# Two of four Hadamard fold quarters from sums and differences formed on VectorE, and the down-weight transform placed behind the first gate of tile 2

## What is computed

```python
def fwht(x):                      # Walsh-Hadamard transform over the last dimension, n values
    h = 1
    while h < n:
        a, b = halves(x, h)
        x = stack([a + b, a - b])
        h *= 2
    return x / sqrt(n)

xn = layernorm(x)                                       # x: 8 x 512 x 256
attn = windowed_attention(rope(xn @ Wq), rope(xn @ Wk), xn @ Wv) @ Wo    # 32 heads, 8 kv heads, window 128
y = fwht(xn * SU_ug) / SCALE
up = y @ W_up.T * (Wscale_ug[:INTER] * SCALE)           # INTER = 1024, HIDDEN = 256
gate = y @ W_gate.T * (Wscale_ug[INTER:] * SCALE)
h = fwht(silu(gate) * up * SU_dp) / SCALE
out = x + attn + h @ W_down.T * (Wscale_dp * SCALE)
```

## Time and profile before

| | |
|---|---|
| median of 3 runs | 1272.94 us (1270.57 to 1273.37) |
| the profiled execution | 1271.77 us, span 1269.8 us |
| TensorE busy | 1248.3 us, 98% of the span |
| VectorE busy | 908.3 us, 72% |
| ScalarE busy | 784.9 us, 62% |
| GpSimd busy | 641.6 us, 51% |
| the chain that ended last | 81% TensorE, 8% VectorE, 6% ScalarE, 2% the queue of SP |
| granted TensorE clock | 1.00 in every slice |

### The profile page before, as it was taken

One profiled execution on the slowest core, in us unless ns is written; L12 is line 12 of the kernel. 1 busy time (PEld: TensorE's weight loads), 2 busy tenths in 40 slices (PEclk: granted clock), 3 DMA queues, 4 the chain that ended last, 5 costly groups with the idle time before them and its releaser, 6 DMA issues.

```text
span 1269.8 us, 38064 instructions
## 1 busy us (share of the span) xinstructions
PE 1248.3 (98%) x14574; PEld 1059.4 (83%) x14574; DVE 908.3 (72%) x1617; ACT 784.9 (62%) x2862; POOL 641.6 (51%) x655
## 2 busy tenths in 40 slices
PE   8999999999999999999999999999999999999997
PEld 4788888888888888888888888888888888888886
DVE  5878875788647886488855888558884688745875
ACT  3477762777628775387744867457673677626775
POOL 5346652466425654266641766327653276524663
PEclk9999999999999999999999999999999999999999
DMA  6415535144152342434332343314424144241431
GB/s 225 122 52 175 167 105 150 54 127 135 40 150 78 110 132 64 121 102 128 92 98 86 111 134 93 113 55 124 125 90 129 61 115 154 63 133 36 135 99 51
DMA packets 72354, 137.56 MB, mean 108 GB/s; under 512 B 15600, under 2 KB 29424, under 8 KB 72176
## 3 DMA queue, kind: packets, MB, share of 16 engines
q1 hardware_dynamic: 71040, 134.41, 35.5%
q10 hardware_dynamic: 1136, 0.73, 0.2%
HBM read 72.17 MB, written 12.58 MB: 67 GB/s over the span
## 4 chain that ended last, share of the span: by engine, by line
PE 81%; DVE 8%; ACT 6%; SPq 2%; issue 2%; DMA 1%; DVEq 0%; ACTq 0%
PE PROJ L978 15%; PE PROJ L980 14%; PE PROJ L979 14%; PE S L1134 9%; PE TR L1148 8%; PE O L1165 5%; ACT e_sb L646 4%; PE O L1177 4%; PE TR L1165 4%; PE S L980 2%; PE S L979 2%; PE S L978 2%; DVE negmax L893 2%; DVE prod L780 1%; DVE o_lo L736 1%
## 5 line engine op out<-in xcount | busy, mean ns | idle before, releaser
L646 ACT ACTIVATE e_sb<-S,negmax 128x128 f32<-128x128 f32 x1024 | 363.9, 381 | 27.3 <-DVE negmax L893 24.9
L514 POOL TENSOR_TENSOR e_sb<-e_sb,rinv 128x512 f32<-128x512 f32 x256 | 264.1, 1040 | 44.4 <-DVE rinv L898 44.1
L522 POOL TENSOR_SCALAR_AFFINE_SELECT p_cur<-pt_sb 128x512 f32<-128x512 f32 x192 | 122.4, 639 | 259.2 <-ACT pt_sb L656 258.4
L656 ACT ACTIVATE pt_sb<-TR 128x512 f32<-128x512 f32 x256 | 154.3, 603 | 130.9 <-PE TR L1148 130.6
L646 ACT ACTIVATION_READ_ACCUMULATOR e_sb<-S,negmax 128x1 f32 x1024 | 225.3, 220 | 0.0
L780 DVE TENSOR_TENSOR prod<-PROJ,rope_sb 128x1024 f32<-128x1024 f32 x160 | 192.6, 1212 | 43.0 <-PE PROJ L980 39.0
L893 DVE TENSOR_REDUCE negmax<-S 128x4 f32<-128x512 f32 x256 | 176.9, 691 | 8.8
L1134 PE MATMUL S<-k_stack,q_stack 64*64 64x64 f32 (+2 forms) x5632 | 179.9, 266 | 1.4 <-ACT e_sb L646 1.2
L1134 PEld LDWEIGHTS S<-k_stack,q_stack 64*64 64x64 f32 x5632 | 160.2, 133 | 8.6 <-ACT e_sb L646 5.2
L490 POOL TENSOR_TENSOR qy<-prod 128x512 f32<-128x512 f32 x64 | 82.2, 1284 | 161.3 <-DVE prod L780 161.3
L1148 PE MATMUL TR<-ident,e_sb 128*128 128x128 f32 x1024 | 158.9, 278 | 3.6 <-ACT pt_sb L656 3.4
(11 more groups left out here) (105 smaller groups left out, 2876.9 us busy)
## 6 DMA issues: line engine op xcount, KB each, us to landing
q_stack<-qy SPq DMA_DIRECT2D x512, 64.0 KB, 2.1
wq_ring<-wq_split_d SPq DMA_DIRECT2D x56, 512.0 KB, 4.7
wo_ring<-wo_split_d SPq DMA_DIRECT2D x56, 512.0 KB, 3.6
k_stack<-ky SPq DMA_DIRECT2D x256, 64.0 KB, 2.8
x_in<-x SPq DMA_DIRECT2D x8, 512.0 KB, 4.6
wq_split_d<-wq_ring SPq DMA_DIRECT2D x8, 512.0 KB, 4.8
wo_split_d<-wo_ring SPq DMA_DIRECT2D x8, 512.0 KB, 3.6
out<-acc SPq DMA_DIRECT2D x16, 256.0 KB, 4.2
```

What stands on the lines that cost most here:

```text
L514: nc.gpsimd.tensor_tensor(e, e, r, ALU.mult).then_inc(norm_done, 1)
L646: last = nc.scalar.activation(e_sb[:, n % 2, r, :], s_heads(n, 1)[:, r, :], ACT.Exp, bias=negmax[:, n % 2, r:r + 1], accum_out=rowsum[:, n ...
L656: nc.scalar.activation(pt_sb[:, n % 4, :, :], TR[:, :, :], ACT.Copy).then_inc(t_copied, 1)
```

## The change

For the last two quarters (k = 2 and 3) VectorE forms the sum and the difference of the two input halves (`gu_butterfly`), the sum into `acc`, which is not in use yet, the difference in place in `gu_stage`. TensorE then does one fp32 matmul for each half instead of two. The two new pairs stand on VectorE behind `fold_low(3)` and behind `fold_low(5)`. GpSimd waits for the folds before it fills `acc`. `down_weights` moves on TensorE from behind up 1 to behind gate 2, and with it `wd_scale` and `wd_low(0)` on VectorE and `wd_high` on ScalarE move behind the products of q side 1 part 0 and behind the split of hidden tile 1.

```diff
@@ -223,6 +223,10 @@
 
             tokens = o_p[part][:, :, i * P:(i + 2) * P].rearrange("p m (s a q) -> p m s a q", s=2, a=2)
             return tokens[:, :, :, a, :]
+
+        def gu_pair(k):
+
+            return acc[:, :, :].rearrange("p t c -> p (t c)")[:, (k - 2) * 512:(k - 1) * 512], gu_stage[:, 1, k * 512:(k + 1) * 512]
 
         def s_heads(n, which):
 
@@ -253,6 +257,7 @@
         w_hi = sem("w_hi")
         w_lo = sem("w_lo")
         su_done = sem("su_done")
+        gu_sums = sem("gu_sums")
         fold_ready = sem("fold_ready")
         fold_hi = sem("fold_hi")
         fold_lo = sem("fold_lo")
@@ -533,6 +538,8 @@
                     rotate(b, "q", 0)
                 rotate(b, "q", 1)
                 pool.wait_ge(x_loaded, b * 16 + 16)
+                if not b:
+                    pool.wait_ge(fold_ready, CT * 4)
 
                 wait_apart(pool, "pool", out_stored, 2 * b * 16 + 16)
                 nc.gpsimd.tensor_copy(acc[:, :, :], x_in[:, :, :]).then_inc(acc_init, 1)
@@ -675,10 +682,12 @@
                 h_high(0)
                 silu(1)
                 if not b:
+                    h_high(1)
                     for n in range(FT // 2):
                         wd_high(n)
                 for j in range(2, FT):
-                    h_high(j - 1)
+                    if b or j > 2:
+                        h_high(j - 1)
                     silu(j)
                     if not b and j in (3, 5):
                         wo_high(j // 2 - 1)
@@ -807,6 +816,12 @@
                 nc.vector.tensor_tensor(a, PROJ[:, bank, :].rearrange("p (t c) -> p t c", t=2), a, ALU.add
                                         ).then_inc(wo_added, 1)
 
+            def gu_butterfly(k):
+                first, second = (gu_stage[:, c, k * 512:(k + 1) * 512] for c in range(CT))
+                dve.wait_ge(gu_in[k], 16)
+                nc.vector.tensor_tensor(gu_pair(k)[0], first, second, ALU.add).then_inc(gu_sums, 1)
+                nc.vector.tensor_tensor(gu_pair(k)[1], first, second, ALU.subtract).then_inc(gu_sums, 1)
+
             def fold_low(n):
                 k, c = divmod(n, CT)
                 dve.wait_ge(fold_hi, n + 1)
@@ -833,11 +848,13 @@
             wq_low(0)
             fold_low(2)
             fold_low(3)
+            gu_butterfly(2)
             dve.wait_ge(consts_in, CONSTS * 16)
             products(0, "k", 0, 0)
             products(0, "k", 0, 1)
             fold_low(4)
             fold_low(5)
+            gu_butterfly(3)
             products(0, "q", 0, 0)
             products(0, "q", 0, 1)
             fold_low(6)
@@ -907,15 +924,15 @@
                         wo_add(b - 1, NKV - 1, 1)
                 if not b:
                     wq_low(1)
-                    for n in range(FT // 2):
-                        wd_scale(n)
                 for j in range(2, FT):
                     n = j // 2
                     if j in (2, 4):
                         products(b, "q", n, 0)
+                        h_low(j - 1)
                         if not b and j == 2:
+                            for k in range(FT // 2):
+                                wd_scale(k)
                             wd_low(0)
-                        h_low(j - 1)
                         products(b, "q", n, 1)
                     else:
                         h_low(j - 1)
@@ -1044,12 +1061,18 @@
                 last.then_inc(proj_ready, 1)
 
             def fold_gate_up(k):
-                pe.wait_ge(gu_in[k], 16)
+                if k < 2:
+                    pe.wait_ge(gu_in[k], 16)
                 for c in range(CT):
                     n = k * CT + c
                     if n >= 4:
 
                         pe.wait_ge(fold_lo, n - 3)
+                    if k >= 2:
+                        pe.wait_ge(gu_sums, n - 2 * CT + 1)
+                        nc.tensor.matmul(S4[:, n % 4, :], had[:, 0, :], gu_pair(k)[c], start=True, stop=True
+                                         ).then_inc(fold_ready, 1)
+                        continue
                     for cc in range(CT):
                         last = nc.tensor.matmul(S4[:, n % 4, :], had[:, c * cc, :], gu_stage[:, cc, k * 512:(k + 1) * 512],
                                                 start=cc == 0, stop=cc == CT - 1)
@@ -1187,14 +1210,14 @@
                             if alternate:
                                 project(b, "q", n, part)
                             hidden(name, j)
+                            if not b and j == 2 and not part:
+                                down_weights()
                             if b and not j and name == "gate":
                                 values_mixed(b - 1, STEPS // 2 - 1)
                         if b and j == 1:
                             project_out(b - 1, NKV - 1, 1)
                         if j >= 2:
                             down(j - 2)
-                    if not b and not n:
-                        down_weights()
                 down(FT - 2)
                 values(0)
                 down(FT - 1)
```

## The result

| | before | after |
|---|---|---|
| median | 1271.06 us (8 runs, 1269.71 to 1274.59) | 1276.93 us (8 runs, 1274.77 to 1279.45) |
| ratio | | 1.0042, 95% interval 1.0033 to 1.0051 |
| the profiled execution | 1271.77 us, span 1269.8 us | span 1274.8 us |
| TensorE busy | 1248.3 us | 1247.9 us |

The change makes the kernel slower by 0.42%, 5.3 us (5.9 by the medians of the table). The forecast was 1276.8 us and slower. It named the place, the lock between VectorE and GpSimd, and the order of the waits, and all of that stands in the trace. But its +3.9 us was too small for this stage, where the trace shows +6.6: of the difference, 1.6 us is TensorE's clock, which the forecast had as a rival and not as a term.

What follows compares the result with a forecast made beforehand. TensorE, busy 98% of the span, was taken to bound the kernel. The 3.43 us saved is lost to waits and up 2 starts 3.9 us late: 1272.94 + 3.9 = 1276.8 us, range 1272.6 to 1279.0.

Steps and rivals of the forecast that it cites:

- the lock between VectorE and GpSimd: VectorE instructions with both inputs in SBUF never overlap GpSimd's; they take turns, a 512-wide one costing 0.55 us after its wait.
- (a): TensorE folds: two quarters lose two fp32 matmuls of four each, saving 3.43 us if nothing is late.
- (b): First VectorE pair: sum ends at 18.49, difference at 21.29; products of k start at 21.2, and the first saving is gone.
- (c): Second VectorE pair: sum ends at 25.5, difference at 27.2; some 0.3 of 3.43 us left, or 2 us late without its turn.
- (d): GpSimd's butterfly, delayed by the later rotation and three turns given to VectorE, ends at 36.95 instead of 32.52.
- (e): Second q weight tile: wq_low(1) waits for the butterfly and ends at 37.5, so TensorE stands 3.5 us before q side 1.
- (f): Moved down weights: silu of tile 2 waits behind scalings and last high part; up 2 starts at 46.25, not 42.35, +3.9 us.
- (g): Parts that cost nothing; behind up 2 no TensorE gap could fill the shift except attention's 2.5 us.
- The rival of 2.5 us: Attention of row 0 takes back some of the loss, up to its 2.5 us of gaps: 1274.3, chance 0.12.
- The rival of the clock: TensorE's clock falls in the 3.5 us gap ahead of q side 1, costing 1.7 us more: 1278.5, chance 0.12.
- The price in the Trainium skill: VectorE's fp32 tensor_tensor takes 691 ns at 512 columns whatever GpSimd does; would give the no-lock rival, 1273.2, chance 0.14.

Runs made afterwards that it cites:

- no_pool_butterfly: The change with the three butterfly levels on GpSimd left out, so the down weights go unmixed across tiles; ratio 0.9996, stage 61.81 us.
- kept_busy: The change with three fp32 matmuls of unused result added on TensorE ahead of q side 1 part 0; ratio 1.0036, stage 65.87 us.
- wq_early: The change with the split of the second q weight tile brought forward, behind fold_high(5) and fold_low(7); ratio 1.0035, stage 66.70 us.
- silu_first: The change with silu of tile 2 put ahead of the four high parts of the down weights on ScalarE; ratio 1.0031, stage 66.08 us.
- before_again: The kernel before, unchanged, run once more for its trace; stage 60.98 us, row 0 takes 156.06 us between the additions to acc.
- one_pair: The kernel before with a sum-and-difference pair for the last quarter only, placed in a gap of VectorE; ratio 0.9984, stage 60.22 us.
- move_alone: The kernel before with only the down weights moved behind gate 2; ratio 1.0023, stage 63.82 us.
- no_vector_pairs: The change without the four new VectorE instructions, TensorE reading the raw halves of the last two quarters; ratio 1.0003, stage 62.93 us.
- pairs_alone: The change with the down weights, their scaling and high parts back in their old places; ratio 1.0032, stage 66.19 us.

## Why the prediction was right, and where it was too small

- **(a) The saving of 3.43 us**: the folds' shorter matmuls are there, two records each instead of four. Right.
- **(b) First pair**: worked out 18.49 and 21.29 for the ends, measured 18.62 and 21.38; the products of k start at 21.30 (worked out 21.2). Right to 0.1 us. no_pool_butterfly shows that GpSimd's work beside it makes it.
- **(c) Second pair**: worked out 25.5 and 27.2, measured 25.56 and 27.24. The sum did get its turn.
- **(d) The butterfly**: worked out 36.95, measured 37.08.
- **(e) The second q tile**: worked out a gap of 3.5 us, measured 3.46. kept_busy fills it to 0.9 us, and wq_early removes it by the order.
- **(f) Silu behind the high parts**: worked out 46.25 for up 2, measured 48.56. silu_first shows that the wait was rightly named, but two terms were mis-sized. The clock, left out of the sum, is 1.6 us (kept_busy). The other 0.7 is in the eight scalings, which I took as 3.2 us (41.7 to 44.9): in kept_busy, at the full clock, they run from 41.80 to 45.68. Six of them take 2.58 us, one pair for each 0.86 us of a down-weight matmul, and then VectorE stands 0.42 us ahead of the last two; what for, the profile does not show. In wq_early, where these matmuls are long done (41.22), all eight take 3.22 us without a gap. A further 0.16 is in the comparison itself: 42.35 in the chain is where the matmul ahead of up 2 ended, and up 2 had started at 42.19 before. With the 0.2 us by which fold 1 started earlier in the trace after, these are the 2.7 us between +3.9 and +6.6.
- **(g) No term for the rest of the kernel**: the attention of row 0 took back at most 0.4 us (155.68 us in the change, 156.06 in before_again), which is within the 155.7 to 156.4 of the other kernels. The rival of 2.5 us looked right in the first pair of profiles and falls with before_again.
- **The rival of the clock**, at 0.12, happened together with the forecast, priced at 1.7 us and measured at 1.6. By the prediction's own list, a granted clock under 1.00 between 34 and 45 was a sign of being wrong, and up 2 near 46.3 one of being right: on both the trace went against it. The price came from rows that do not show a low clock: over the six records of 4.24 us the windows of the profile give 1.00, so that it fits the measured price is in part luck. It was not a rival but a consequence: the forecast itself made the gap of 3.5 us, and the chance should have been weighed as a term of it. The Trainium skill ("TensorE: Matmul & The Clock Gate", "What's actually happening") was the only source for it ahead of the runs; the windows at 0.80, 0.50 and 0.84 now agree with it.
- **The price in the Trainium skill** ("VectorE: DVE Perf Modes", the TRN2 errata, 691 ns): right with GpSimd idle (0.68 to 0.70 us), too low by up to a factor of 4 beside it (2.84 us).

The total is within its range, and slower for the reason given, though the sum was too small by the clock and by the scalings. The kernel's +5.3 (4.2 to 6.5) meets the stage's +6.6 only at the upper end of its interval. What stays open: why the ratios of most kernels come out about 1 us better than their stages, one_pair's too. From the mark of the stage to the end, the two traces of the kernel before take 1196.1 and 1195.4 us and those of the other kernels 1194.5 to 1196.2, so the rest of the kernel varies between traces by more than that.

## What to carry to other kernels

Work taken from a saturated engine is a gain only if what replaces it, and all that queues behind the replacement, is ready when the engine arrives: place it in a gap in which the engine it takes turns with is idle as well, and follow the delayed neighbour to its last reader. A matmul stretch that is moved away from a place was also the cover of whatever is finished during it (move_alone: 1.7 us). And when a plan opens a gap of some microseconds on TensorE, price the lower clock behind it as part of the plan.

## What the runs showed of the hardware that I had not expected

- Gaps of TensorE of 2.7, 2.8, 3.3 and 3.5 us (no_vector_pairs, pairs_alone, wq_early, the change) were each followed by a granted clock of 0.50; gaps up to 1.7 us (move_alone) were not. The clock did not fall in the gap but behind it, 0.3 us after work was taken up again in pairs_alone (36.99, 37.3) and 1.4 us after it in the change (37.78, 39.2), and it came back by itself under full work. So the price falls on the matmuls behind the gap.
- Two VectorE instructions with both inputs in SBUF in a row do not keep the turn: GpSimd's waiting instruction goes between them (the sum ends at 18.62, GpSimd at 20.83, the difference at 21.38). So a pair beside a chain of 2.4 us instructions costs 3.8 us (17.60 to 21.38), nearly three times its own 1.3.
